# A router without ties, constants for columns, and a new order of steps in a fused audio tower

## The reference, cut to what matters

```python
expert_logits = softmax(relu(features @ router_w1 + router_b1) @ router_w2 + router_b2)
top_w, top_i = jax.lax.top_k(expert_logits, 2)
routing_weights = softmax(top_w)
combined = sum(take_along_axis(expert_out, top_i) * routing_weights[..., None])
```

## Time and profile before

| | |
|---|---|
| runs | 646.14, 648.12, 648.10 us, median 648.1 us |
| the profiled execution | span 644.8 us; its own device time isn't among what was recorded |
| mean granted TensorE clock | 0.983 |
| TensorE busy | 572.2 us, 89% of the span |
| VectorE busy | 540.6 us, 84% |
| ScalarE busy | 525.0 us, 81% |
| GpSimd busy | 423.5 us, 66% |

### The profile page before, as it was taken

One profiled execution on the slowest core, in us unless ns is written; L12 is line 12 of the kernel. 1 busy time (PEld: TensorE's weight loads), 2 busy tenths in 40 slices (PEclk: granted clock), 3 DMA queues, 4 the chain that ended last, 5 costly groups with the idle time before them and its releaser, 6 DMA issues.

```text
span 644.8 us, 22886 instructions
## 1 busy us (share of the span) xinstructions
PE 572.2 (89%) x9531; PEld 302.5 (47%) x9531; DVE 540.6 (84%) x1019; ACT 525.0 (81%) x1044; POOL 423.5 (66%) x549
## 2 busy tenths in 40 slices
PE   3777778999999999999999999999999999999972
PEld 2333234545455555455445455455545545545431
DVE  5898999999899899989898999999898987764441
ACT  1345668989899999998898998999999888888761
POOL 7758899788867677768567766767686755423110
PEclk9998879999999999999999999999999999999998
DMA  3432222221220213230211212220221001000001
GB/s 78 83 82 63 65 59 59 61 52 31 52 48 20 56 43 77 47 74 14 69 31 45 55 44 61 58 47 15 68 49 29 5 8 31 17 14 14 2 14 29
DMA packets 77575, 28.52 MB, mean 44 GB/s; under 512 B 69271, under 2 KB 77463, under 8 KB 77463
## 3 DMA queue, kind: packets, MB, share of 16 engines
q1 hardware_dynamic: 71290, 25.92, 17.6%
q10 hardware_dynamic: 6173, 1.05, 0.9%
HBM read 13.25 MB, written 3.05 MB: 25 GB/s over the span
## 4 chain that ended last, share of the span: by engine, by line
PE 44%; ACT 19%; DVE 17%; POOL 9%; issue 5%; DMA 2%; ACTq 2%; SPq 1%; POOLq 0%; DVEq 0%
PE ring L1274 7%; PE ring L1353 5%; ACT pm L1057 5%; PE ring L1366 4%; PE ring L1461 4%; DVE ring L1714 3%; PE ring L1260 3%; PE ring L1432 2%; PE ring L1441 2%; ACT hid L1100 2%; PE ring L1229 2%; PE ring L1249 2%; PE ring L1336 1%; PE ring L1412 1%; DVE carry_C L1710 1%
## 5 line engine op out<-in xcount | busy, mean ns | idle before, releaser
L1057 ACT ACTIVATE pm<-ring,two_col 93x744 f32<-93x744 f32 x128 | 107.4, 873 | 10.0 <-PE ring L1353 9.0
L1353 PE MATMUL ring<-q_exp,qk 32*93 32x372 f32 x512 | 56.4, 507 | 7.7 <-ACT ln_rows_a L1021 1.1
L1821 DVE TENSOR_TENSOR hidw<-hid,ring 128x744 f32<-128x744 f32 x48 | 44.3, 922 | 19.1 <-PE ring L1422 11.5
L911 POOL TENSOR_TENSOR q_exp<-qk,mask_q 128x1488 f32<-128x1488 f32 x16 | 42.9, 2683 | 22.2 <-DVE qk L1772 22.2
L1366 PE MATMUL ring<-pm,v 97*32 97x93 f32 x2048 | 53.7, 245 | 1.2 <-ACT pm L1057 0.4
L1100 ACT ACTIVATE hid<-ring,b_col 128x372 f32<-128x372 f32 x96 | 49.3, 568 | 1.5 <-PE ring L1441 0.9
L1366 PEld LDWEIGHTS ring<-pm,v 97*32 97x32 f32 x2048 | 42.4, 109 | 15.3 <-ACT pm L1057 3.4
L1107 ACT ACTIVATE hid<-ring,b_col 128x744 f32<-128x744 f32 x48 | 42.2, 879 | 8.9 <-PE ring L1432 6.4
L1432 PE MATMUL ring<-hid,w 64*64 64x372 f32 x384 | 40.3, 489 | 3.2 <-ACT hid L1100 2.7
L896 POOL TENSOR_TENSOR base_C<-base_C,carry_C 128x744 f32<-128x744 f32 x16 | 28.5, 1781 | 20.1 <-DVE carry_C L1723 9.5
L1441 PE MATMUL ring<-nrm_f,w 64*64 64x372 f32 x384 | 40.0, 486 | 0.2
(11 more groups left out here) (368 smaller groups left out, 1755.4 us busy)
## 6 DMA issues: line engine op xcount, KB each, us to landing
xin_A<-in_x_dram SPq DMA_DIRECT2D x62, 93.0 KB
xin_B<-in_x_dram SPq DMA_DIRECT2D x62, 93.0 KB
x_A<-x_A SPq DMA_DIRECT2D x32, 93.0 KB, 2.4
x_B<-x_B SPq DMA_DIRECT2D x32, 93.0 KB, 2.2
x_C<-x_C SPq DMA_DIRECT2D x32, 93.0 KB, 2.2
out_dram<-osb SPq DMA_DIRECT2D x15, 186.0 KB
x_D<-x_D SPq DMA_DIRECT2D x32, 46.5 KB, 2.2
w<-in_L_ffn_expert_w_dram SPq DMA_DIRECT2D x6, 48.0 KB
```

Source lines behind the costliest of these rows:

```text
L1057: a.activation(pm[q % 2][h][0:TOUT].rearrange("m a j n -> m a (j n)"), out_of(f"att.s{q}{h}", g)[0:TOUT, :, 0:COLS], ACT.Square, bias=two_ ...
L1353: ins = mm(o[h][0:TOUT, b, 0:COLS], qk[r:r + 32, 1, q * TOUT:(q + 1) * TOUT], q_exp[r:r + 32, q].rearrange("p j n -> p (j n)"), start=True ...
L1821: tt(hidw[k][:], hid2[:], out_of(f"ffn.g_{k}", g)[:, :, 0:COLS], ALU.mult).then_inc(me, 1)
```

## The change

The router of the main path loses the treatment of ties. `oh0` is one where the shifted logit is at least zero, computed by GpSimd in a new step `first`; `rest` is the probability where it is below; `oh1` is one where `rest` is at its maximum. A token with a tie would get more than two ones. GpSimd adds both one-hots of all groups into `ties`; if a row's sum is over 2 x 8 x 16, the flag is raised and the general path, which keeps the treatment of ties, computes everything. The work tensors `logit`, `prob`, `rest` now lie in SBUF, and `ffn.lg`'s bank is free after `route1`. The flag now waits for the last `ties`; `prep.flags:15` stands between `ffn.hidw2:15` and `ffn.fin:15`, `prep.flag:15` last on TensorE, `prep.again:15` last on VectorE.

Three bias columns are constants now. An entry of TensorE's text with `!` (767 of 1000) asks for its bank ahead of everything else. All five texts are new: 261 steps of TensorE have another bank, ScalarE's begins with `prep.l2`, `prep.l3`, `prep.l5`, SyncE's with `prep.l0`, `l1`, `l4`. Near the end, TensorE's `oT:14` stands ahead of `g_2:15` where it stood behind, and ScalarE's `out:14` ahead of `hid2_2:15`.

```diff
-            "pe": ("prep.w0:0/0 A.xT:0/2 prep.w1:0/1 A.row:0/0 B.xT:0/2 B.row:0/2 prep.qkvp:0/0 A.z:0/2 B.dpre:0/4 "
+            "pe": ("prep.w0:0/0 prep.w2:0/7 B.xT:0/2 A.xT:0/4 B.row:0/6 B.z:0/4 A.row:0/2 B.dpre:0/0 prep.w1:0/5! B.s:0/0! "
...
-                 "dve ffn.top": ["sum", "rsum", "key0", "kmax0", "oh0", "rest", "m1", "eq1", "key1", "kmax1", "oh1", "diff"],
-                 "pool ffn.split": ["w1", "w", "gate", "hi", "mid", "rest", "lo"]}
+                 "dve ffn.top": ["sum", "rest", "rsum", "m1", "diff", "oh1"],
+                 "pool ffn.split": ["w1", "w", "gate", "hi", "mid", "rest", "lo", "both", "ties"]}
...
             def experts(g_, u, s):
+                if s == "first":
+                    need(g_, "dve ffn.shift")
+                    need(g_, "pool ffn.ties", back=1)
+                    if g_ < NG:
+                        g.tensor_scalar(oh0[:], logit[:], 0.0, None, ALU.is_ge).then_inc(me, 1)
...
+                    g.tensor_tensor(both[:], oh0[:], oh1[:], ALU.add).then_inc(me, 1)
+                    need(g_, "pool ffn.both")
+                    g.tensor_tensor(ties[:], ties[:], both[:], ALU.add).then_inc(me, 1)
...
-                    a.activation(ln_rows[w][:], out_of(f"{u}.var", g)[:, 0, 0:TOUT], ACT.Ln, bias=eps_col[:]).then_inc(me, 1)
+                    a.activation(ln_rows[w][:], out_of(f"{u}.var", g)[:, 0, 0:TOUT], ACT.Ln, bias=LN_EPS).then_inc(me, 1)
...
-                    a.activation(qk_norm[:], qk_norm[:], ACT.Exp, bias=ln_col[:], scale=-0.5).then_inc(me, 1)
+                    a.activation(qk_norm[:], qk_norm[:], ACT.Exp, bias=12.0 * LN2, scale=-0.5).then_inc(me, 1)
...
-                                 bias=two_col[0:TOUT], scale=0.5 ** 0.5).then_inc(me, 1)
+                                 bias=2.0, scale=0.5 ** 0.5).then_inc(me, 1)
...
-                    a.activation(pr, lg, ACT.Exp).then_inc(me, 1)
+                    need(g, "dve ffn.sum", "dve ffn.rest", back=1)
+                    a.activation(prob[:], logit[:], ACT.Exp).then_inc(me, 1)
...
             def do(g, u, s):
+                if (f"{u}.{s}", str(g)) in FIRST:
+                    for job in PAIRED.get(f"{u}.{s}", (f"{u}.{s}",)):
+                        bank(g, job)
...
+                    need(g, "pool ffn.ties")
+                    v.tensor_reduce(tie_sum[:], ties[:].rearrange("m b e -> m (b e)"), AX_X, ALU.add).then_inc(c, 1)
+                    dve.wait_ge(c, 8)
+                    ts(tie_sum[:], tie_sum[:], 2.0 * GB * NG + 0.5, None, ALU.is_gt).then_inc(c, 1)
+                    dve.wait_ge(c, 9)
+                    tt(flag_sum[0:TOUT], flag_sum[0:TOUT], tie_sum[:], ALU.add).then_inc(c, 1)
+                    dve.wait_ge(c, 10)
...
-                    step(v.tensor_reduce(st[:, 1], pr, AX_X, ALU.add), "sum")
-                    step(v.reciprocal(rsum, st[:, 1]), "rsum")
-                    step(stt(key, lg, 0.0, rank[:], ALU.is_ge, ALU.mult), "key0")
-                    step(v.tensor_reduce(st[:, 7], key, AX_X, ALU.max), "kmax0")
-                    step(tt(oh0[:], key, spread(st[:, 7]), ALU.is_equal), "oh0")
-                    step(stt(pr, oh0[:], -4.0, pr, ALU.mult, ALU.add), "rest")
-                    step(v.tensor_reduce(st[:, 4], pr, AX_X, ALU.max), "m1")
-                    step(tt(key, pr, spread(st[:, 4]), ALU.is_ge), "eq1")
-                    step(tt(key, key, rank[:], ALU.mult), "key1")
-                    step(v.tensor_reduce(st[:, 7], key, AX_X, ALU.max), "kmax1")
-                    step(tt(oh1[:], key, spread(st[:, 7]), ALU.is_equal), "oh1")
-                    stt(st[:, 5], st[:, 4], -1.0, rsum, ALU.add, ALU.mult).then_inc(me, 1)
+                    v.tensor_reduce(st[:, 1], prob[:], AX_X, ALU.add).then_inc(me, 1)
+                    if g < NG:
+                        stt(rest[:], logit[:], 0.0, prob[:], ALU.is_lt, ALU.mult).then_inc(me, 1)
...
+                    need(g, "dve ffn.sum")
+                    v.reciprocal(st[:, 7], st[:, 1]).then_inc(me, 1)
+                    need(g, "dve ffn.rest")
+                    v.tensor_reduce(st[:, 4], rest[:], AX_X, ALU.max).then_inc(me, 1)
+                    need(g, "dve ffn.m1")
+                    need(g, "act ffn.topexp", back=1)
+                    stt(st[:, 5], st[:, 4], -1.0, st[:, 7], ALU.add, ALU.mult).then_inc(me, 1)
+                    need(g, "pool ffn.w1", "pool ffn.both", back=1)
+                    if g < NG:
+                        tt(oh1[:], rest[:], spread(st[:, 4]), ALU.is_ge).then_inc(me, 1)
```

More of the change, by code:

```diff
@@ L195, in audio_tower @@
         st = sb("st", [TOUT, 8, GB])
+        logit, prob, rest, key, ties, both = (sb(n, [TOUT, GB, NX]) for n in ("logit", "prob", "rest", "key", "ties", "both"))
+        tie_sum = sb("tie_sum", [TOUT, 1])
         gate = sb("gate", [TOUT, GB, NX])
@@ L567, in audio_tower @@
                  "att.nrow": (1, "act att.nln"), "att.proj": (1, "dve att.mid"),
-                 "ffn.rh": (2, "act ffn.rh"), "ffn.lg": (1, "dve ffn.top"), "ffn.gT": (1, "act ffn.gateT"),
+                 "ffn.rh": (2, "act ffn.rh"), "ffn.lg": (1, "dve ffn.route1"), "ffn.gT": (1, "act ffn.gateT"),
                  "ffn.o": (1, "dve ffn.fin"), "ffn.oT": (1, "act ffn.out")}
@@ L591, in audio_tower @@
         ATT_STEPS += ["pe nrow", "act nln", "act rec", "pe nb0", "dve att0", "pe nb1", "dve att1", "pe proj", "dve mid"]
-        FFN_STEPS = NORM_STEPS + ["pe rh", "act rh", "pe lg", "dve route1", "act prexp", "dve top",
+        FFN_STEPS = NORM_STEPS + ["pe rh", "act rh", "pe lg", "dve route1", "pool first", "act prexp", "dve top",
                                   "act topexp", "act topln", "act toprec", "pool split", "pe gT", "act gateT"]
@@ L605, in entries @@
             return [(w, int(g)) for w, g in (entry.split("/")[0].split(":") for entry in text.split())]
+        FIRST = {tuple(entry.split("/")[0].split(":")) for entry in ORDER["pe"].split() if entry[-1] == "!"}
         MAIN = {who: entries(ORDER[who]) for who in ORDER}
@@ L640, in audio_tower @@
             w_, g_ = step_.split(":")
-            BANK |= {(job, int(g_)): int(b) for job, b in zip(PAIRED.get(w_, (w_,)), banks_.split(","))}
+            BANK |= {(job, int(g_)): int(b) for job, b in zip(PAIRED.get(w_, (w_,)), banks_.rstrip("!").split(","))}
         BEFORE = {}
@@ L1794, in step @@
                     need(g, f"dve ffn.{name}")
-                if s in ("route1", "top"):
-                    lg, pr, key, rsum = (router(g, k) for k in ("lg", "pr", "key", "rsum"))
                 if s == "route1":
                     need(g, "pe ffn.lg")
+                    lg = logits_made(g)
                     step(v.tensor_reduce(st[:, 0], lg, AX_X, ALU.max), "mx")
-                    tt(lg, lg, spread(st[:, 0]), ALU.subtract).then_inc(me, 1)
+                    need(g, "act ffn.prexp", "dve ffn.rest", "pool ffn.first", back=1)
@@ L1816, in experts @@
-                    stt(st[:, 5], st[:, 4], -1.0, rsum, ALU.add, ALU.mult).then_inc(me, 1)
+                    v.tensor_reduce(st[:, 1], prob[:], AX_X, ALU.add).then_inc(me, 1)
+                    if g < NG:
+                        stt(rest[:], logit[:], 0.0, prob[:], ALU.is_lt, ALU.mult).then_inc(me, 1)
+                    else:
+                        need(g, "pool ffn.w", "pool ffn.ties", back=1)
+                        chosen(g, oh0, "first", stt(key[:], logit[:], 0.0, rank[:], ALU.is_ge, ALU.mult))
+                        dve.wait_ge(sem("ties_first"), 3 * (g - NG) + 3)
+                        stt(rest[:], oh0[:], -4.0, prob[:], ALU.mult, ALU.add).then_inc(me, 1)
@@ new lines, in experts @@
+                    if g < NG:
+                        tt(oh1[:], rest[:], spread(st[:, 4]), ALU.is_ge).then_inc(me, 1)
+                    else:
+                        q = sem("ties_more")
+                        tt(key[:], rest[:], spread(st[:, 4]), ALU.is_ge).then_inc(q, 1)
+                        dve.wait_ge(q, g - NG + 1)
+                        chosen(g, oh1, "second", tt(key[:], key[:], rank[:], ALU.mult))
+                        dve.wait_ge(sem("ties_second"), 3 * (g - NG) + 3)
+                        v.memset(tick[:, 13:14], 0.0).then_inc(me, 1)
```

30 lines of the change are left out of this document (16 added, 14 removed), and 628 rows, old and new, of the table ORDER.

## The result

| | before | changed |
|---|---|---|
| median of the runs | 647.12 us (645.2 to 648.12) | 682.27 us (678.52 to 683.49) |
| ratio, 95% interval | | 1.0534 [1.051, 1.0558] |
| span of the profiled execution | 644.8 us | 676.6 us |
| mean granted TensorE clock | 0.983 | 0.951 |

The account below looks back on a forecast made before the run. Three engines near full: VectorE bounds the ramp, TensorE the body, a dependent chain the end. Terms +5 - 6.5 - 1.6 = -3.1 us took the span from 644.8 to 641.7; plus 3.3 gave 645.0 us, range 637 to 653.

Parts of the forecast that it names:

- The body: 120 to 615 us: lighter ScalarE and VectorE cut TensorE's waiting, 5 us, plus 1.5 from reordering; -6.5, bounds -1 and -16.
- the tail: Last stores: shorter router and earlier oT:14 and out:14 bring the last osb sooner; -1.6 us, bounds +0.5 and -3.
- in inverse ratio: Body: as ScalarE's and VectorE's idle time grows, TensorE's waiting shrinks by a quarter, 5 of 21.4 us.
- a sign of being wrong: Body: the prediction would be wrong if TensorE's idle time stayed at 21 us or fell under 10.
- The start: Ramp: 11.9 us of ScalarE issues delay B.x:0 to about 26.2 and B.scan:0 to 41.6; +5 us, bounds 0 and 8.7.
- both orders hold about 20.5 us of VectorE work: Ramp, from B.scan:0 to C.scan:0: equal VectorE work in old and new order, so C.scan:0 comes near 63.5 for 58.01.
- Three memsets less: Start: three memsets fewer and one more lie beside the wait for the first loads; nothing.
- 3.3 us between span and time: Whole kernel: median of runs 648.1 lies 3.3 us above its span; added to span 641.7 to give 645.0.
- Bank waits first: TensorE: 767 of 1000 steps ask for the bank ahead of the data; zero taken, -3 to +4 us kept.
- the exclusion: Rival, chance 0.08: VectorE's two-tensor SBUF router steps and GpSimd exclude each other, eating the 1.87 us a group; 649.5 us.
- the flag's steps hidden: Tail: 1.9 us of flag steps between hidw2:15 and fin:15 lie beside 2.4 us of matmuls; uncovered, up to 1.9.
- The late start decides: Rival, chance 0.20: start +8, body gives 2, tail -1; 653 us. Condition: start costs over 5 us more than body returns.

Follow-up runs that it names:

- old_head: Changed kernel with SyncE's whole old order, the other four engines' old first steps, and three unused tiles restoring the old addresses; 637.5 us, 0.9843 of before.
- old_orders_aligned: Changed code under all five old orders and banks, with three unused tiles restoring the old addresses; 646.9 us, 0.999 of before.
- stand-in router: Run on old_head: bias columns back and six more dependent VectorE steps in each router, result unused; 669.4 us, 1.0338 of before.
- late_issues: Changed kernel with ScalarE's three preparation issue steps put back into its waits; 678.6 us, 1.0497 of before.
- late_sync_head: Changed kernel with SyncE's whole old order, ScalarE's three preparations late and three unused tiles; 652.8 us, 1.0073 of before.
- head_mended: late_sync_head with TensorE's B.z:0 moved behind B.dpre:0 and ScalarE's prep.l2 and prep.l5 moved later; 654.4 us, 1.0117 of before.

## Why the prediction was wrong

The chain of medians takes the difference apart, each link one of the edits above: old_head 637.5; new beginning +14.5 (652.0); addresses +3.4 (655.4); issues early on ScalarE +3.1 (658.5); SyncE's order +23.8 (682.3). From before to old_head it is -9.6. The links come from kernels with four or more runs each, on different chips; the medians of before on these chips lie 1.1 us apart, so a link is good to about 1 us.

- *The body and the tail, -6.5 and -1.6.* The sum, -8.1, is near: old_head is 9.6 us under before, and the end alone gave 2.4. That is luck in good part, for the reason was half wrong. The prediction gave the relief 5 us by itself, "in inverse ratio", and the reordering 1.5. By itself the relief gives nothing (old_orders_aligned: TensorE idle for 22.3 us of the body, 21.4 before); to texts that are planned for it it is worth some 32 us (an upper figure, since the stand-in router is longer than the old one), and those texts without it are slower than before (669.4 for 648.2). Even in old_head TensorE's idle time of the body is 21.0 us, which the prediction itself had named as a sign of being wrong. The step that failed is the ratio: idle time of VectorE and ScalarE doesn't shorten TensorE's in an unchanged order, where the steps stand at places chosen for the old durations.
- *No term for SyncE's order.* This is the main failure, 23.8 of the 35 us (19.5 in old_head). "All five texts are new" stood in the change, and only four of them were priced, SyncE's in its first entries alone. The traces of before showed what to look at: `A.load:14` led its use by 37 us, the load directly behind a store took 7.48 us to issue, and all groups share one `osb`. In the changed kernel TensorE waited for three loads, each directly behind a store, and two swaps between 120 and 640 us, and ScalarE 5.3 us for a store.
- *The start, +5.* `B.x:0` was right to 0.4 us, and late_issues shows that this was the smaller thing: 3 to 4 us. `B.scan:0` missed by 3.4 us: `row_w` took 4.99 us under GpSimd where it takes 0.52 free of it, though the earlier trace rows had shown the same pair held. Then "both orders hold about 20.5 us of VectorE work" failed: the fifth scan is 17.8 us late. The new beginning costs 14.5 us with the issues and SyncE's entries put back. It lies in the order of the four engines together; two places that looked like its cause (late_sync_head, head_mended) were not, so which wait carries it stays open.
- *"Three memsets less ... nothing."* True of the memsets; the tiles themselves moved all addresses, 3.4 to 8.9 us. Nothing in the trace of before bounds that.
- *3.3 us between span and time.* Every run whose span is on record shows 1.7 to 2.0 (678.52 and 676.6 for the changed kernel), so the 645.0 stood about 1.5 us too high.
- *Bank waits first, zero; the exclusion, 0.08; the flag's steps hidden.* The first two are right: 652.2 for 652.0, and 0.14 us a group. The general path didn't run, and the new end with the flag's steps in it gained; the flag's steps alone were not measured.
- *The rivals.* "The late start decides" had the right sign at 653 and the right place, but a seventh of the size. Its condition was met, and still it isn't the main cause: the start alone, 17.6 us, would have given 637.5 + 17.6 = 655.1.

Of the 44.8 us between old_head and the changed kernel, 27.2 had no term and 17.6 a term of 5; the gain that was set against them came out near, and its reason did not.

## What to carry to other kernels

Price every text of a new order, the DMA queue's first: for each load, swap and store ask how far it is issued ahead of its use, what stands directly ahead of it, and what stands behind it when it is late. The busy shares can't show this, the lead of a transfer in the trace of before can. A relief of engines that aren't the bound is worth what the order makes of it, so test the code under the old order and the order under the old code apart. When tiles are added or dropped, compare the addresses of the rest, and measure with unused tiles in their place.
